# A vision tower's last stage: a choice of expert moved ahead of a mixing, two normalised rows turned inside expert pairs, and the last expert pair in two banks

## The reference, cut to what matters

```python
h = h + 0.5 * (y_fwd + y_bwd)            # y = (scan output * silu(z)) @ out_w.T
x = layernorm(h)                         # over the 256 values, no gain
scores = einsum('bsh,eh->bse', x, gate_w)
onehot = one_hot(argmax(scores), 8)
expert_out = einsum('bsh,efh->bsef', x, expert_w)
h = h + x + einsum('bsef,bse->bsf', expert_out, onehot)
```

## Time and profile before

| | us |
|---|---|
| median of 3 runs | 508.62 |
| lowest and highest run | 506.94, 511.68 |
| the profiled execution's own time | 510.66 |
| its span, from the first to the last instruction | 508.9 |
| TensorE busy (matmuls) | 456.6 (90%) |
| VectorE busy | 371.9 (73%) |
| ScalarE busy | 238.7 (47%) |
| GpSimd busy | 167.5 (33%) |

### The profile page before, as it was taken

The page is one execution under the profiler, slowest core; times in us unless marked ns, Lnnn a source line. Parts: engine busy times, 40 slices in busy tenths (PEclk is TensorE's granted clock), DMA queues, the critical chain, the costliest instruction groups (busy, mean ns, idle before and its releaser), DMA issues.

```text
span 508.9 us, 6819 instructions
## 1 busy us (share of the span) xinstructions
PE 456.6 (90%) x1782; PEld 222.9 (44%) x1782; DVE 371.9 (73%) x704; ACT 238.7 (47%) x422; POOL 167.5 (33%) x163
## 2 busy tenths in 40 slices
PE   6899999999999999899777867988889889799997
PEld 3554555655555566444444422222222222384653
DVE  0246586566565778453799898899999999988654
ACT  1053423122222321466978856788888888411100
POOL 6000100100100111403542005889899898340000
PEclk9899999999999999998879987899999999999999
DMA  9982029200000000400217572456555664610000
GB/s 256 309 274 86 1 75 308 59 1 0 0 2 0 0 1 0 144 13 0 79 41 217 141 222 82 141 165 193 162 156 158 197 171 135 172 49 11 12 10 21
DMA packets 36135, 51.73 MB, mean 102 GB/s; under 512 B 5858, under 2 KB 26670, under 8 KB 36112
## 3 DMA queue, kind: packets, MB, share of 16 engines
q1 hardware_dynamic: 34960, 50.26, 33.8%
q10 hardware_dynamic: 1152, 1.19, 0.7%
HBM read 34.59 MB, written 16.52 MB: 100 GB/s over the span
## 4 chain that ended last, share of the span: by engine, by line
PE 32%; DVE 8%; DMA 5%; SPq 5%; issue 4%; ACT 4%; POOL 1%; ACTq 0%; DVEq 0%; POOLq 0%
PE ps L1976 6%; PE ps L1639 4%; PE ps L1953 4%; DMA brows<-bparts 3%; PE ps L955 3%; PE ps L962 3%; PE ps L1590 3%; PE ps L1603 2%; PE ps L1612 2%; SPq L1528 1%; PE ps L1621 1%; SPq L1455 1%; DVE rc L1309 1%; PE ps L994 1%; DVE da L1815 1%
## 5 line engine op out<-in xcount | busy, mean ns | idle before, releaser
L1783 POOL TENSOR_TENSOR gb<-da,hb 128x512 f32<-128x512 f32 x62 | 77.8, 1276 | 52.1 <-ACT da L1703 45.5
L1703 ACT ACTIVATE da<-da 128x512 f32<-128x512 f32 x128 | 78.9, 629 | 23.5 <-DVE da L1815 21.4
L1815 DVE TENSOR_TENSOR da<-ps,expA 128x512 f32<-128x512 f32 x128 | 84.0, 685 | 5.8 <-PE ps L1590 5.0
L321 PE MATMUL ps<-xbuf,convw 128*128 128x384 f32 (+1 forms) x220 | 74.9, 494 | 1.9 <-DMA xbuf<-in_xT 1.9
L366 PE MATMUL ps<-wall,peT 128*128 128x512 f32 x144 | 67.7, 593 | 0.0
L1590 PE MATMUL ps<-drows,selb 96*128 96x512 bf16 x128 | 48.5, 401 | 9.2 <-DVE da L1815 5.5
L321 PEld LDWEIGHTS ps<-xbuf,convw 128*128 128x128 f32 (+1 forms) x220 | 42.0, 194 | 30.4 <-issue 2.6
L1603 PE MATMUL ps<-urows,brows 96*128 96x512 bf16 x96 | 35.4, 396 | 12.4 <-DVE gb L1822 7.8
L539 ACT ACTIVATE kvs<-ps 128x512 f32<-128x512 f32 x36 | 21.5, 597 | 51.9 <-PE ps L366 51.9
L531 ACT ACTIVATE peT<-ps 128x384 f32<-128x384 f32 x24 | 11.8, 490 | 68.5 <-PE ps L321 61.6
L1783 POOL TENSOR_TENSOR gb<-da,gb 128x512 f32<-128x512 f32 x30 | 37.8, 1282 | 0.0
(11 more groups left out here) (234 smaller groups left out, 768.5 us busy)
## 6 DMA issues: line engine op xcount, KB each, us to landing
xbuf<-in_xT SPq DMA_DIRECT2D x11, 768.0 KB
yscr<-yst SPq DMA_DIRECT2D x28, 208.0 KB
brows<-bparts SPq DMA_DIRECT2D x16, 240.0 KB, 3.0
dparts<-pt SPq DMA_DIRECT2D x21, 128.0 KB, 2.4
drows<-dparts SPq DMA_DIRECT2D x14, 192.0 KB, 2.8
uparts<-pt SPq DMA_DIRECT2D x18, 128.0 KB, 2.4
urows<-uparts SPq DMA_DIRECT2D x16, 144.0 KB, 2.7
inw<-in_in_wT SPq DMA_DIRECT2D x2, 1024.0 KB
```

Of the source, the lines that this page charges most:

```text
L321: mm = pe.matmul(bank(T_EMB + j % 2, 0, EN), convw[0:n, k, h * P:(h + 1) * P], xbuf[0:n, q, k, c * EN:(c + 1) * EN], start=(k == 0), stop= ...
L1703: act.activation(da_at(q, j), da_at(q, j), ACT.Exp, scale=-1.0).then_inc(da_ready, 1)
L1783: pool.tensor_tensor(gb_at(q, j), da_at(q, j), state, ALU.mult).then_inc({2: m2_done, 3: m3_done, 4: m4_done}[s_], 1)
L1815: dve.tensor_tensor(da_at(q, j), bank(j % 2), expA[:, j % 2, :], ALU.mult).then_inc(e_free, 1)
```

## The change

It has three parts, all in the last stage; no buffer and no arithmetic changes.

1. On VectorE, the choice of the second token goes in front of the mixing of the third, which is then done in the middle of that choice, after two of its four pairs (midway). The other mixings keep their places: mixed(3) behind chosen(1), mixed(4) behind chosen(2).
2. On TensorE, x_turned(3) and x_turned(4) go into experts(2) and experts(3), ahead of the last pair (k = 3) and behind its wait for ex5_used. projected(4) stays behind experts(2), so the gate of the fourth token then follows the projection, and that of the fifth the last pair of the fourth.
3. The last pair (m = 19) is computed as two experts of 256 columns each, the first in bank 5 as before, the second in bank 0. Each raises ex5_ready, and VectorE's second addition waits for the second.

```diff
+        LAST_PAIR = L * E8 // 2 - 1
+
+        def pair_half(m, e):
+            if m == LAST_PAIR and e == 1:
+                return bank(0, 0, C)
+            return bank(4 + m % 3, e * C, (e + 1) * C)
...
                     if m >= 3:
                         pe.wait_ge(ex5_used, m - 2)
+                    if k == E8 // 2 - 1 and n + 1 in (3, 4):
+                        x_turned(n + 1)
+                    if m == LAST_PAIR:
+                        for e in range(2):
+                            for h in range(CH):
+                                mm = pe.matmul(pair_half(m, e), xfT[:, n % 2, h, :],
+                                               expw[:, h, (2 * k + e) * C:(2 * k + e + 1) * C],
+                                               start=(h == 0), stop=(h == CH - 1))
+                            mm.then_inc(ex5_ready, 1)
+                        return
...
             for n in range(L):
-                if n >= 1:
+                if n in (1, 2):
                     x_turned(n)
...
-            def chosen(n):
+            def chosen(n, midway=None):
...
                     for e in range(2):
-                        ins = dve.scalar_tensor_tensor(out=mo[:, n, :], in0=bank(4 + m % 3, e * C, (e + 1) * C),
+                        if m == LAST_PAIR and e == 1:
+                            dve.wait_ge(ex5_ready, m + 2)
+                        ins = dve.scalar_tensor_tensor(out=mo[:, n, :], in0=pair_half(m, e),
...
+                    if midway and k == 1:
+                        midway()
                 dve.sem_inc(mo_ready, 1)
...
-            for n in range(L):
-                chosen(n)
-                if n == 0:
-                    gated(4)
-                if n + 2 < L:
-                    mixed(n + 2)
+            chosen(0)
+            gated(4)
+            chosen(1, lambda: mixed(2))
+            mixed(3)
+            chosen(2)
+            mixed(4)
+            chosen(3)
+            chosen(4)
```

## The result

| | before | after |
|---|---|---|
| median of 20 runs each, us | 509.47 | 506.05 |
| lowest and highest | 506.65, 512.31 | 503.82, 509.21 |
| span of the profiled execution | 508.9 | 504.0 |
| start of the first token's expert matmuls | 457.06 | 455.30 |
| end of the last weighted addition | 506.65 | 501.80 |

The ratio of the times is 0.9935, with a 95% interval from 0.9915 to 0.9955: 3.3 us less, give or take 1.0. The prediction was 3.1 less, a median of 505.5 within 503.3 to 508.0. The median after lies 0.55 above the forecast, for the one before does too: 509.47 of twenty runs, where the forecast started from 508.62 of three.

The account below looks back on a forecast made before the run. The prediction took TensorE to bound the stage, with three stands and a tail to cut: 1.1 + 1.4 + 0.55 = 3.05, say 3.1 us, taking the median from 508.62 to 505.5 us, range 503.3 to 508.0.

Parts of the forecast that it names:

- the room given for it: Third token's mixing inside the second's choice: normalised row ready with 3 us to spare before its turn.
- Rival 2: Second token's stand of TensorE only moves, to the third row's turn or m = 9: 506.6 us, chance 0.05.
- The gaps: Before the expert loads of the fourth and fifth tokens: 1.29 and 1.30 us fall to 0.34, 0.95 each.
- a drained pipeline: Turns inside the pairs: upper bound 0.5 us each if the change of kind doesn't pipeline, 0.25 taken.
- Rival 1: VectorE takes TensorE's place as the late one in the fourth token, half a microsecond lost: 506.0 us, chance 0.07.
- E + 3.06: Fourth token: E is the projection's end; its scores, which the turn needs, are read 3.06 us later.
- the extra for a shorter lag: Last pair: VectorE starts 0.20 us behind 256-column matmuls, not 0.27, so up to 0.1 more gain.
- The loads: Four extra weight loads of 190 ns in the split last pair, lying wholly beside matmuls, charged nothing.
- Rival 3: Last pair's split: loads don't hide, 4 x 0.19 = 0.76 us against the 0.55 gain; 506.3 us, chance 0.04.
- The sum: Gains of the three parts in the last stage: 1.1 + 1.4 + 0.55 = 3.05 us, say 3.1.
- Rival 4: TensorE's clock is lowered in the last stage, costing 5.1 us: 510.6 us, chance 0.04.

Follow-up runs that it names:

- the small matmuls: Changed kernel with all twenty pairs in matmuls of 256 columns, 76 more weight loads: stage 46.69 us against 46.50.
- the last kernel: Changed kernel with the last expert halved into two stored pieces and the pair before it split in two banks: stage 46.34 us, ratio 0.9937 to the kernel before.

## Why the prediction was right

**What bounds it.** TensorE did, in every kernel: each change of the stage's length but the 0.19 of the small matmuls is a stand of TensorE that came or went, or the additions behind its end.

**Part 1,** 1.1 forecast, 1.10 measured alone. The mixing moved into the choice had the room given for it: the third row's turn did not wait. Moved behind the choice it has none, and 0.48 comes back. Rival 2 falls.

**Part 2,** 1.4 forecast, 1.48 measured. The gaps went as worked out, 1.29 and 1.30 to 0.33 and 0.34. The inserted turn costs 0.22, where I had taken 0.25 with 0.5 for a drained pipeline; nothing drains. Rival 1's place was the right one to look at, with 0.29 us of real room against the 0.4 that I gave. It was not used up, so the rival did not come. In the last token I had VectorE 0.02 late and it was 0.13: the step from one token's additions to the next one's scores has an idle of 0.16 that I left out. The next pair takes it up, as forecast. The scores of the fourth token, which the turn needs, I had as read at E + 3.06; that is where their copy starts, and it ends 0.17 later. Here nothing hangs on it.

**Part 3,** 0.55 forecast, 0.50 alone. The term that was mis-sized is the extra for a shorter lag behind matmuls of 256 columns: the last addition starts at 501.32, 0.28 behind 499.32 + 8 x 0.215, as behind 512 columns, and not 0.20. Why the lag is 0.20 behind a projection and 0.28 here stays open. The loads cost nothing that shows. Rival 3 falls with the small matmuls, where the run shows 0.19 for 76 loads. The rule of the Trainium skill's "TensorE: Matmul & The Clock Gate", Part 3, that weight loads overlap running matmuls only where the row groups differ, stands there among the rules for packing small matmuls. For the whole array it would, by an estimate from the loads' 190 ns, have asked for 76 x 0.19 = 14 us, and this trace does not agree with it.

**The sum,** 3.05 forecast, 3.09 in the trace, 3.3 (2.3 to 4.3) in the times. Two errors of 0.05 to 0.08, of opposite sign, nearly cancelled in it, which was luck. The times alone don't tell the sum from the 2.6 of rival 1 or the 2.3 of rival 3; the stages and their waits do.

**Rival 4.** TensorE's granted clock was 1.00 from 455 to the end of the changed kernel's span, by the windows, and 1.00 from 457 to 508 in the kernel before; the denser stage did not lower it:

```profile
455.00:504.00 49.00, 46.21 (x161) 26.45 (x159) 34.21 (x94) 3.71 (x8) 2.98 (x5) 1.00 0.04 14
```

**The spread.** I put the chance of more than 1% at 0.12 for the runs' spread alone; with 20 runs each the ratio stayed within 1% with its whole interval.

## What to carry to other kernels

Where one engine bounds a stage and stands still only in a few places, each stand can be priced from the rows on both sides of it. Here small edits added up as computed, since for each the due time of the next work on every engine had been worked out. A wait is released at the end of the operation that raises the semaphore, and the waiter's own load and step come on top: count 0.1 to 0.3 us less room than start times suggest. When a gain is smaller than the spread of the runs, measure the length of the edited stretch in the trace, not the span.

## What the runs showed of the hardware

- A weight load of the whole array for a float32 matmul lies beside running matmuls: 76 loads more cost 0.19 us together, 2.5 ns each, though each is 190 ns long.
- Two float32 transposes between 512-column matmuls cost their own 0.22 us and no drain.
- A weighted addition from PSUM (float32, 128 partitions) takes 484 ns for 256 columns and 348 for 128.
- A last store of two times 64 KB landed no sooner than one of 128 KB: 2.20 us behind the last addition in both (and 3.86 in the one profile of the last kernel, unexplained). The second one is issued only when SyncE has issued the first, 0.37 us later.
